# Layer 1 of a four-layer network kernel: attention operands and the gated FFN put into one stage ahead of attention

## The reference

```python
def _L1_attn_ref(x, wq, wk, wv, wo, ...):
    q = (x @ wq.T).reshape(B, T, NH, 2, HH)            # NH = 8 heads, in two halves of HH = 16
    k, v = ...                                         # v: 8 heads of 32
    q1, q2, k1, k2 = rotary(rms_norm(half)) for each   # 32 norms of 16 values in a row of q and k
    y = causal_attn(q1, k1, v) - lam * causal_attn(q2, k2, v)
    return y @ wo.T * 0.8
def _L1_ffn_ref(h, gate_w, up_w, down_w):              # 256 -> 1024 -> 256
    return (silu(h @ gate_w.T) * (h @ up_w.T)) @ down_w.T
```

## Time and profile before

| | us |
|---|---|
| median of three runs | 4488.14 (4483.75 to 4491.97) |
| the profiled execution: its time | 4489.93 |
| its span, first to last instruction | 4487.9 |
| granted TensorE clock, mean share of full speed | 0.899 |
| busy share of the span: PE, DVE, ACT, POOL | 81%, 57%, 41%, 16% |

### The profile page before, as it was taken

One profiled execution on the slowest core, in us unless ns is written; L12 is line 12 of the kernel. 1 busy time (PEld: TensorE's weight loads), 2 busy tenths in 40 slices (PEclk: granted clock), 3 DMA queues, 4 the chain that ended last, 5 costly groups with the idle time before them and its releaser, 6 DMA issues. The chain is left out here.

```text
span 4487.9 us, 60794 instructions
## 1 busy us (share of the span) xinstructions
PE 3615.0 (81%) x22476; PEld 2133.6 (48%) x22476; DVE 2573.0 (57%) x5320; ACT 1819.6 (41%) x2736; POOL 729.0 (16%) x894
## 2 busy tenths in 40 slices
PE   5876787768669878798783888988988898898897
PEld 3424334234153634536353566655653663663672
DVE  5756656557474464544536464454665664764764
ACT  2262461542656264452632434443126226216206
POOL 3012111120120000100001232232210220220220
PEclk8988888889889889899896899989999999999999
DMA  5412314123140000000002000002000000000000
GB/s 187 122 40 77 112 34 130 59 80 115 34 141 1 10 20 1 29 1 29 1 1 82 1 29 29 5 24 78 1 1 29 1 1 29 1 1 29 1 1 10
DMA packets 147077, 176.97 MB, mean 39 GB/s; under 512 B 16384, under 2 KB 123392, under 8 KB 146688
## 3 DMA queue, kind: packets, MB, share of 16 engines
q1 hardware_dynamic: 139008, 153.81, 10.9%
q0 software_dynamic: 6144, 16.79, 1.1%
q10 hardware_dynamic: 1632, 2.49, 0.2%
HBM read 126.40 MB, written 51.38 MB: 40 GB/s over the span
## 5 line engine op out<-in xcount | busy, mean ns | idle before, releaser
L708 DVE TENSOR_REDUCE arena<-ps 128x2 f32<-128x1024 f32 (+3 forms) x768 | 698.8, 953 | 160.4 <-PE ps L676 98.2
L906 ACT ACTIVATE arena<-ps 128x1024 f32<-128x1024 f32 (+3 forms) x768 | 576.8, 812 | 161.8 <-PE ps L813 114.1
L989 DVE TENSOR_TENSOR arena<-arena,tri 128x256 f32<-128x256 f32 x512 | 210.2, 423 | 354.1 <-ACT arena L906 322.5
L813 PE MATMUL ps<-arena 64*128 64x512 f16 (+3 forms) x1536 | 260.9, 354 | 165.7 <-ACT arena L906 99.2
L830 PE MATMUL ps<-arena 128*17 128x512 f32 (+3 forms) x3072 | 349.5, 529 | 6.4 <-DVE arena L989 4.0
L465 PE MATMUL ps<-arena,xn_t 128*128 128x512 f32 (+1 forms) x768 | 299.9, 543 | 53.2 <-PEq L65 38.7
L906 ACT ACTIVATE attention<-ps 128x1024 f32<-128x1024 f32 (+3 forms) x384 | 287.9, 809 | 134.6 <-PE ps L813 134.5
L813 PEld LDWEIGHTS ps<-arena 64*128 64x128 f16 x1536 | 71.1, 94 | 522.5 <-ACT arena L906 401.7
L2418 ACT ACTIVATE arena<-ps 128x256 f32<-128x256 f32 x192 | 63.7, 381 | 620.1 <-PE ps L2360 574.8
L830 PE MATMUL ps<-attention 128*33 128x512 f32 (+3 forms) x1536 | 292.1, 504 | 0.0
L676 PE MATMUL ps<-arena 64*128 64x512 f16 (+3 forms) x1536 | 236.2, 334 | 52.5 <-DVE arena L708 37.8
(11 more groups left out here) (323 smaller groups left out, 6632.8 us busy)
## 6 DMA issues: line engine op xcount, KB each, us to landing
arena<-w_experts SPq DMA_DIRECT2D x128, 256.0 KB
acc<-sums SPq DMA_DIRECT2D x16, 1024.0 KB, 5.7
x_next<-sums SPq DMA_DIRECT2D x16, 1024.0 KB, 8.3
arena<-slots_x SPq DMA_DIRECT2D x32, 512.0 KB, 4.5
slots_y<-arena SPq DMA_DIRECT2D x32, 512.0 KB, 4.3
sums<-acc SPq DMA_DIRECT2D x24, 512.0 KB, 2.9
making<-basis SPq DMA_DIRECT2D x16, 768.0 KB, 7.2
slots_x<-arena SPq DMA_DIRECT2D x1, 4096.0 KB, 28.0
```

What stands on the lines that cost most here:

```text
L708: dve.reduce_max(a.mp[:, 2 * j:2 * j + 2, qt, c], out[:, :, 0:w], AX.X).then_inc(self.pair_out, 1)
L813: last = pe.matmul(m.ps[:, 4 + 2 * (v % 2) + odd, q0:CH], a.k[half, pair, kt * P:(kt + 1) * P], a.q[half, pair, c * CH + q0:(c + 1) * CH], ...
L906: act.activation(a.p[:, v % ring, :, q0:CH], m.ps[:, b:b + 2, q0:CH], ACT.Exp, scale=HD ** -0.5).then_inc(exped, 1)
L989: dve.tensor_tensor(diag, diag, keep, ALU.min).then_inc(masked, 1)
```

## The change

The three stages become two. `operands_and_gated` does the work of stages 1 and 3; then comes `attention(..., store=into[2])`, which now stores the sums and normalises the next batch. In the joint stage the gated FFN goes in 32 units of 256 rows (`QT`) instead of 16 of 512: unit n = 8q + i, for a quarter q of the rows. Gate and up products of a unit share one PSUM bank; banks 4 and 5 take turns. Tile t of the attention operands is strung along the units: projection at n = 3t, squares at 3t+1, their sums at 3t+2, root at 3t+3, rotation at 3t+4, high and low parts at 3t+6, transposes at 3t+9, store at 3t+10. `down(q)` runs behind unit 8q+9. The low part of the gated product moves from DVE to POOL.

```diff
-                with place(f"attention1_{b}", rest) as data:
-                    a = attention_memory(m, Arena(data), NM // 2, 2 * HD, NM // 2, 6)
-                    attention_operands(nc, m, a, wqkv, None, turn, True, NM // 2, 2 * HD, (early_in, early_done), into[1], b)
-                    attention(nc, m, a, 2, 64, wo, 1.0 - LAMBDA_INIT, b)
-                with place(f"ffn1_{b}", rest - FFN_PARTS) as data, place(f"ffn_parts1_{b}", FFN_PARTS, F32R) as parts:
-                    gated_ffn(nc, m, gated_memory(data, parts), wg, wu, wd, b, into[2])
+                        operands_and_gated(nc, m, a, *projection_memory(words, parts), wqkv, turn, (early_in, early_done),
+                                           wg, wu, wd, into[1], b)
+                    with place(f"attention1_{b}", rest - live_words) as words:
+                        attention_scratch(a, Arena(words), NM // 2, 6)
+                        attention(nc, m, a, 2, 64, wo, 1.0 - LAMBDA_INIT, b, store=into[2])
...
+PROJECT_AT = (0, 3, 6, 9, 12, 15, 18, 21)
+H_SLOTS = 12
...
             def up(n):
-                c, i = divmod(n, ni)
+                q, i = divmod(n, ni)
                 if n >= 2:
                     pe.wait_ge(gated, n - 1)
...
-                        last = pe.matmul(m.ps[:, 2 * (n % 2) + j, :], w[wp][:, k, i * P:(i + 1) * P],
-                                         f.x[:, xp, k, c * CH:(c + 1) * CH], start=(k, (wp, xp)) == terms[0],
+                        last = pe.matmul(m.ps[:, 4 + n % 2, j * QT:(j + 1) * QT], w[wp][:, k, i * P:(i + 1) * P],
+                                         f.x[:, xp, k, columns(q)], start=(k, (wp, xp)) == terms[0],
...
             for n in range(units):
+                if tile_at(n, 0) is not None:
+                    project(tile_at(n, 0))
                 up(n)
+                if tile_at(n, 9) is not None:
+                    turn(tile_at(n, 9))
+                if n % ni == 1 and n >= ni:
                     down(n // ni - 1)
...
             for n in range(units):
+                act.activation(f.gate[:, n % 2, :], m.ps[:, 4 + n % 2, 0:QT], ACT.Silu).then_inc(silued, 1)
                 if n >= 1:
                     split(n - 1)
+                for behind, step in ((1, square), (3, root), (6, stack_high), (10, store)):
+                    if tile_at(n, behind) is not None:
+                        step(tile_at(n, behind))
...
             for n in range(units):
+                join(n)
+                for behind, piece in ((0, take), (2, mean_squares), (4, rotate)):
+                    if tile_at(n, behind) is not None:
+                        piece(tile_at(n, behind))
...
+            for n in range(units):
+                pool.wait_ge(high, n + 1)
+                pool.tensor_tensor(f.h[:, 1, n % H_SLOTS, :], f.inter[:, n % 3, :], f.h[:, 0, n % H_SLOTS, :].bitcast(F32),
+                                   ALU.subtract).then_inc(low, 1)
```

More of the change, by code:

```diff
@@ L1052, in gated_memory, with operands_and_gated, tile_at, sums @@
     ar = Arena(parts)
     f.x = ar.take(2, KD, S, dtype=F32R)
-    f.h = ar.take(2, 2, F1 // P, CH, dtype=F32R)
-    return f
-def gated_ffn(nc, m, f, wg, wu, wd, batch, store):
+    f.h = ar.take(2, H_SLOTS, QT, dtype=F32R)
+    return a, f
+def operands_and_gated(nc, m, live, a, f, wqkv, table, weights, wg, wu, wd, src, batch):
+    gh, heads, vd, half = 2 * NM, NM // 2, 2 * HD, HD // 2
     ni = F1 // P
[L1063 to L1068, removed]
+    units = NQ * ni
+    products = [(0, 0), (0, 1), (1, 0)]
+    cos, sin = (v.rearrange("p (h c) -> p h c", c=HD) for v in table)
+    def tile_at(n, behind):
+        return PROJECT_AT.index(n - behind) if n - behind in PROJECT_AT else None
+    def sums(t):
+        return m.small[:, (t % 2) * gh:(t % 2 + 1) * gh]
+    def roots(t):
+        return m.small[:, (2 + t % 2) * gh:(3 + t % 2) * gh]
+    def slots(stack, t):
+        return stack[:, t % 2, :].rearrange("p (h s c) -> p h s c", h=NM, c=HD)
+    def heads_of(t):
+        return a.qk[:, t % 4, :].rearrange("p (h c) -> p h c", c=HD)
+    def chunk(c):
+        return slice(c * CH, (c + 1) * CH)
+    def columns(q):
+        return slice(q * QT, (q + 1) * QT)
+    with stage(nc, "proj", "taken", "steps", "squared", "rms_in", "rms_std", "rotated", "hi", "stacked", "turned", "stored",
+               "cleared", "x_high", "x_low", "upped", "silued", "gated", "high", "low", "downed", "added", pool=True) as \
+            (block, proj, taken, steps, squared, rms_in, rms_std, rotated, hi, stacked, turned, stored,
+             cleared, x_high, x_low, upped, silued, gated, high, low, downed, added):
@@ L1070, in _, with project @@
         @block.sync
         def _(sp):
-            sp.sem_clear(m.acc_in)
-            ahead.sync_end(sp)
-            store_sums(sp, m, store, batch, added)
+            begin_batch(sp, m, src, batch)
         @block.tensor
         def _(pe):
+            def project(t):
+                if t >= 1:
+                    pe.wait_ge(taken, 2 * t)
+                for j, (c0, w) in enumerate(((0, 512), (512, 256))):
+                    for k in range(KD):
+                        last = pe.matmul(m.ps[:, j, 0:w], m.xn_t[:, k, t * P:(t + 1) * P], wqkv[:, k, c0:c0 + w],
+                                         start=(k == 0), stop=(k == KD - 1))
+                last.then_inc(proj, 1)
@@ L1089, in up, with down @@
                                          stop=(k, (wp, xp)) == terms[-1])
[L1090 to L1098, removed]
+                last.then_inc(upped, 1)
+            def down(q):
+                pe.wait_ge(low, ni * (q + 1))
+                if q >= 2:
+                    pe.wait_ge(added, 2 * (q - 1))
+                for j in range(QT // P):
+                    terms = [(i, p) for i in range(ni) for p in products]
@@ new lines, in split, with square, root @@
+                act.activation(f.h[:, 0, n % H_SLOTS, :], f.inter[:, n % 3, :], ACT.Copy).then_inc(high, 1)
+            def square(t):
+                act.wait_ge(taken, 2 * t + 1)
+                if t >= 2:
+                    act.wait_ge(rotated, t - 1)
+                act.activation(a.t1[:, t % 2, :], a.qk[:, t % 4, :], ACT.Square).then_inc(squared, 1)
+            def root(t):
+                act.wait_ge(rms_in, t + 1)
+                act.activation(roots(t), sums(t), ACT.Sqrt).then_inc(rms_std, 1)
```

187 lines of the change are left out of this document (124 added, 63 removed).

## The result

The changed kernel takes 4464.53 us (median of 4 runs, 4460.87 to 4468.33) against 4487.03 (4483.75 to 4491.97): ratio 0.9938, 95% interval 0.9923 to 0.9953. It is faster, by 22.5 us where I forecast 69. The profiled execution is the longest of the four, 4468.33 us with a span of 4466.6.

The account below looks back on a forecast made before the run. It took PE as busiest but no engine full, with stages bound by waits between in-order queues. Joint stage 113.1, attention 138.9 and boundaries 3.5 made 255.5 us a batch against 273.0, so 4420 us; range 4370 to 4470.

Parts of the forecast that it names:

- tail wait: Joint stage's end: Silu, split, store, low part and latencies with nothing over them before the last down, 3.6 us.
- the loop through the engines: Joint stage: PE's next units wait for products behind table loads and rotation, 9.1 us; two cycles at least 16.2.
- 8.2 a cycle: Joint stage, one row tile: three units, a projection and a turn on PE take 8.2 us; ACT's sum is 7.8.
- unknown (c): Rotation on DVE beside POOL's pieces: one hit of 0.38 us per cycle, 2.7 a batch, 11 us, left in the range.
- rival C: Little gain: joint-stage cycles near 10 us because three equally loaded queues rarely meet without gaps, 4450 to 4479 us; chance 0.17.
- own signs of being wrong: Projections starting over 10 us apart, PE's clock dropping inside the joint stage, or attention growing by over 8 us.
- The root: Attention, block 10: the next batch's normalisation root falls between exponentials and costs 2.6 us that can't be made up.
- The four turns: Attention, blocks 12 to 15: PE part of the next batch's normalisation, 4 x 1.03 = 4.1 us, where PE is full.
- The warm start: Attention's start: a dense down in front keeps the clock up, giving back 1.5 of 2.2 us lost.
- Boundaries: Between stages: PE's start and POOL's drain, 1.5 and 2.0 us, 3.5 for two; one of three is gone.
- B: PE-bound: the loop hides and the kernel takes 4355 to 4385 us; chance 0.12.
- D: Slower: cycle over 10.7 us through ACT's 16 table loads, if a pair's switch cost another 2.5 us; chance 0.08.

Follow-up runs that it names:

- the kernel with the copy: Changed kernel with a plain copy in place of the square root between the Silus, so no table load: 4402.66 us, ratio 0.9835.
- the first three experiments: Each against the changed kernel: gated low parts cut to 8 columns, 0.9907; gated low part on DVE, 0.9904; plain copy for the root, 0.9835.
- the tail experiment: Changed kernel with the last high part put ahead of the last store of q and k at the stage's end: 4335.51 us, ratio 0.9902.
- Both edits: Changed kernel with the gated product's low part on DVE and a plain copy in place of the square root: 4288.44 us, ratio 0.9791.
- the combined ones: Changed kernel with low part on DVE, table-free inverse root on POOL, last high part before last store: three Newton steps 0.9822, two 0.9794.
- the changed kernel's second profile: The changed kernel run once more without an edit: 4453.57 us, beside 4478.26 for the kernel before.
- its third timing: The changed kernel unedited, timed again beside the combined versions on one chip: 4351.19 us against 4380.35 for the kernel before, ratio 0.993.

## Why the prediction was wrong

The direction, the place of the gain and most terms held. The size did not: 7.3 us a batch instead of 17.5. By the terms of the prediction, for batch 1:

| term | forecast | measured |
|---|---|---|
| start, and units 1 to 3 with a projection | 14.2 | 13.6 |
| units 4 to 21, with `down(0)` and `down(1)` | 61.6 | 65.4 |
| units 22 to 25 and `down(2)` | 16.4 | 20.3 |
| units 26 to 31 | 10.8 | 10.6 |
| tail wait | 3.6 | 3.65 |
| `down(3)` | 5.8 | 7.5 |
| attention to its last add | 138.9 | 139.7 |

**The step that failed is the loop through the engines** ("Two cycles thus take at least 16.2 us, 8.1 each", and 10.6 for units 22 to 25). The prediction had the right pieces in it, loads, parts, Silu, products and rotation, and summed them to 9.1 us. But it closed the loop over PE, and so spread these 9.1 over two row tiles. The loop closes in one tile and without PE: the root of the next tile stands on ACT behind a high part, that high part waits for a product, and that product stands on DVE behind this tile's rotation. So the prediction's own pieces already make a round of about 9 us, longer than PE's 8.2, and the round measured is 10.2 us. What changes the pieces changes the round: 10.2 becomes 9.4 with 0.8 us less of rotation, and 9.1 with 1.5 less and a low part more.

The larger cost in this loop is the table loads: the kernel without them is 11 us a batch shorter. The prediction took 8.2 a cycle, which is PE's own sum, so in the cycles it charged the loads nothing; for the whole stage it had 113.1 against 105 if nothing but PE counted. A pair takes what the earlier trace rows shows; the error is in what the pair delays. Successive projections of the changed kernel start 9.5, 6.8, 9.1, 8.6, 7.9, 13.6 and 7.8 us apart (`down`'s 5.8 taken off where one lies between), the last six 9.0 on average; 6.8 and 7.8 are also the shortest in the kernel with the copy, so PE's own pace without and with a turn. In units 22 to 25, where no projection covers it, the loop shows its bare length: from 1651.72 to 1661.93, 10.2 us for three units. From the end of unit 21 to that of unit 25 the prediction had 10.6; it took 14.6, and 10.6 in the kernel with the copy.

The smaller term is the rotation, put in at 3.3, which takes 4.8. That is the unknown (c), POOL beside DVE. The 3.3 was already untypical of the kernel before: the earlier trace rows has a median of 1.07 for the first product against 0.69, so most rotations there took 3.7. I took the 0.38 between them for the size of a hit. It is what was left of a POOL piece when the product began:

```profile
1587.46 0.67 POOL L604 TENSOR_TENSOR attention<-attention 128x256 f16<-128x256 f32 x1
...
1587.61 1.07 DVE L519 TENSOR_TENSOR attention<-attention,small 128x512 f32<-128x512 f32 x1
```

The product ends at 1588.68, 0.55 us after POOL's piece (1588.13), as in all 28 such rotations. In the joint stage three or four of POOL's pieces fall on most rotations, and the sum is 1.46. In the batch it comes to 2.7 to 3.2 us net of the moved pieces, what the small hit was priced at too, by luck; and it was left out of the sum.

The time lies in rival C (cycles near 10 us, 4450 to 4479), which I had given 0.17. Its reason, three queues that rarely meet without gaps, is not what the runs show: the round of 10.2 us is fixed by the order of two queues. Of the prediction's own signs of being wrong, one gap between projections was over 10 us (13.6), and PE's clock did drop inside the stage.

**down(3)** was put at full clock; after a wait of 3.65 its clock falls to the low level for its first microseconds and it takes 1.7 more. The wait itself was right to 0.05, and the tail experiment shows that both shrink together. The same happens inside the stage. Before unit 24 PE waits 1.87 us, and its twelve matmuls take 2.84 us instead of 1.7, at a granted clock of 0.52. Before unit 16 it waits 1.81, and the twelve of unit 17 take 2.64, at 0.55.

**Attention** was right in sum (139.7 for 138.9), partly by luck. The root is 2.5 for 2.6. The four turns show as 2.6, not 4.1: the 1.03 us of the earlier trace rows are eight transposes, which is two turns, and a batch has 16 transposes and not 32. The warm start gives 0.7 back, not 1.5. Against these stands the end, from the last score to the last add, which is 1.5 longer than in the kernel before, at a lower clock. **Boundaries** are 4.0 for 3.5.

**Layer 0** took 10.6 us longer in the profiled run of after than in that of before, on code that the change leaves alone; in the seven kernels from "Both edits" to the combined ones, the changed one among them, layer 0's attentions start 273 to 275.3 us apart, in the first profiles 296 to 307.5. In the changed kernel's second profile and the first three experiments, all on one other chip, it is 296 to 300. So the difference is largest from chip to chip. The batches of layer 1 give 29 us in every profile of the changed kernel, and so does its third timing. That the 22.5 of the first comparison are lower through layer 0 fits its profiles; what makes layer 0 vary from chip to chip and from run to run stays open.

**The rivals.** The batch of 255.5 that I forecast is what the kernel gives without its table loads (254.8). B (4355 to 4385 of 4490, a ratio of 0.970 to 0.977) was reached by no version. D's mechanism was half right: the loads are what costs, but by their number on the loop, not by a dearer pair.

The changed kernel's timeline has 3.9 us from the first load to the next Silu, with root and q and k parts between. The Trainium skill's rule in "ScalarE: Activation LUTs", on what ACT_TABLE_LOAD costs, of 2.66 for every switch, would make it over 6; it does not hold here.

The pieces of DVE and POOL that overlap end one after the other, as shown above, and a DVE piece of 0.69 takes 1.05 beside one of POOL. By the rule on DVE and GpSimd in the Trainium skill's "SBUF — State Buffer" ("Who interferes with whom") a DVE instruction with two SBUF inputs and a GpSimd instruction that reads SBUF block each other in full, and the trace agrees. The prediction read its 0.38 as agreeing in part only; that was the misreading. DVE's copies out of PSUM keep their time beside POOL (L499 takes 0.41 under L603).

## What to carry to other kernels

A loop through several in-order queues is found by asking, piece by piece, behind what it stands on its own engine and for what it waits on another, until one comes back to the same piece of the next round; its length is then compared with each engine's sum. The sums alone do not show it: what is added to a queue that is 60% busy can come back one for one (DVE: 18.8 us more busy, 18.3 longer). Before a table-switching function is put between two of another table, price it per use in the loop, and look for a form without a table on an engine off the loop: a chain of two steps there beat one of three by 3 to 4 us a batch. When work moves to an idle engine, look at which pieces it will run beside, since two that both read SBUF may run one after the other; and where a stage ends on a wait, order the last pieces by what the next matmul needs, since the wait also costs the clock.

## What the runs showed of the hardware that was not expected

- DVE pieces with two SBUF inputs and POOL's pieces run one after the other where they overlap, in all 32 rotations: the rotation goes from 3.32 to 4.78 us, POOL's pieces from 0.67 to 1.13. A DVE piece of 32 columns with one input (L1283) goes from 0.18 to 0.67 and ends 0.04 us after POOL's. With POOL's low parts cut to 8 columns 4.0 us of rotation remain.
- A dependent piece of 32 columns costs 0.23 to 0.29 us on DVE and 0.22 to 0.30 on POOL, so a chain of such pieces is as long on either.
- PE's clock fell, for 1 to 3 us, after waits of 1.81, 1.87, 2.35 and 3.65 us: `down` took 7.48 after 3.65, and 7.40 after 2.35 in the kernel with low parts on DVE, but 5.95 after 2.26 in another. A wait's length alone doesn't say.
